# Mixing layer, second part: squares in place and shorter lags between its stages

## The chip, the cores and the metric

One core of a Trainium2 chip runs the whole program. The time is the device time of one execution in microseconds; the time of a kernel is the median of its runs. Engines: PE (TensorE, matrix products and transposes into PSUM), DVE (VectorE), ACT (ScalarE), POOL (GpSimd, no access to PSUM), and SP, which here only issues DMAs. Each engine runs its own list of instructions in order; semaphores tie them together.

## The reference

Four blocks follow each other on `x` (4096 tokens of 128 channels, as 4 sequences of 1024): `x = x + layernorm(block(layernorm(x)))`. The change lies in the first block, a mixing layer with a recurrence, and in the hand-over to the second, a mixture of 16 experts:

```
x = x + r * wkv                                # first part, recurrence over time
h2 = _ln(x, ln2_w, ln2_b)
xx2 = concatenate([h2[:, -1:], h2[:, :-1]])     # shift by one token
xxx2 = h2 + (xx2 - h2) * ts
kc = xxx2 @ Wck.T                              # 128 -> 512
rc = sigmoid(xxx2 @ Wcr.T)
vv = relu(kc) ** 2 @ Wcv.T                     # 512 -> 128
return x + rc * vv
```

Second block: `scores = sigmoid(x @ w_gate.T)`; the best two of four groups of experts, in them the best four experts, their scores normalised to weights; then every expert's `silu(x @ w1.T) * (x @ w3.T) @ w2.T`, weighted and summed, and a shared expert.

## The kernel before, in words

Tokens are worked in 8 groups of 512 (two groups to a sequence); matrices in work are 128 channels by 512 tokens, a PSUM bank each (8 banks). `X` and `XA` hold tokens by rows, `B[0..5]` six buffers of 128 x 4100 (`KF` = `B[2]` keys, `VF` = `B[3]` values, `RF` = `B[4]`, `XXX` = `B[1]`, `MMB` = `B[5]`), `RB` sixteen rows of 512 for short-lived results.

Each engine has a loop `for step in ...` in which a stage of group g runs at step g + lag; the order of the stages in a step is the order of the list of (lag, stage) pairs. "Round" below is one such step. The stages of the second part, with the lines of the profile:

- decay (DVE L870 to L875, ACT L1469 and L1472): exponents for group g from its keys; tanh and exp on ACT.
- wkv (DVE L881 to L898): scan and what follows; it reads the values `VF` and signals `y_b`. Group g + 1 needs group g.
- res: PE transposes y back (L344), DVE adds it to the tokens (L902) and takes the statistics (L799, L803; signals `st0`).
- rstd on POOL (L1769 to L1775; four dependent small instructions, the second a power), norm on ACT (L1413), turn on PE (L344) and ACT (L1476), and for every second group a copy of the last token on DVE (L911) that the shift of that sequence needs.
- mix (DVE L916, L918): shift and blend, signals `xxx_b`.
- kc: PE multiplies by four blocks of Wck and by Wcr (L392, five products; the profile shows two records each). ACT takes relu of the four (L1492) and squares chunks 1 and 3 (L1497), POOL squares chunks 0 and 2 (L1840), ACT takes tanh of the fifth (L1501). Relu goes to half of `B[KF]` (even and odd groups in turn), squares to half of `B[VF]`. Since both hold keys and values of all groups, group 0 waits for `y_b` 4 and group 1 for `y_b` 8.
- vv (PE L405): four products, accumulated. DVE multiplies by the gate (L925, `y2_b`).
- ret: transposed back (L344), added, with statistics (L930, L799); rstd on POOL; add: norm on ACT (L1413), added to `X` on POOL (L1801).
- the expert gate's norm: statistics (`stats_n`), rstd, norm to row 9 of `RB`, turn (PE L344, ACT L1516), gate (PE L428: 16 columns for each 128 tokens).

The choice of experts (`route`, DVE L979 to L1017) is cut into pieces by `yield`; it runs for three ranges of tokens, of which the first is groups 0 and 1, after `score_n` on ACT (L1521, sigmoid). Its weights are transposed on PE (L438), copied (`spread_n`, DVE L1023), sent by SP to DRAM and read back spread over partitions (128 KB a piece) into the four buffers `CW`. POOL's `gated_m` (L1872) multiplies a unit by its weights. A unit (`experts(v)`) is one expert for one group: `gate_up_m` (PE L447, L450), silu (ACT L1530), product (DVE L1037), `gated_m`, and three units later `out_m` (PE L462). Nine units make a group, 72 in all. Units begin at `FIRST_UNIT` = 20 of the loop and run alone after its end at step NG + 15 = 23. After the first four pieces SP also loads the weights and the tables of the third block (896 and 1024 KB) before the piece of unit 4.

The lags before, on PE: res 2, turn 4, kc 8, vv 9, ret 10, turn_n 14, gate_n 15. On DVE and ACT they match.

Of the kernel before, what the change touches and what calls it, by code (L numbers as in the profile page):

```python
# [64 lines left out]
def build(nc, I, out):  # L65
    ctx = ExitStack()
    with ctx:
# [84 lines left out]
        XF = 0  # L152
        small = [SS[:, 512 * i:512 * i + 512].rearrange("p (i e) -> p i e", e=16) for i in range(4)]
# [118 lines left out]
        FIRST_UNIT = 20  # L272
# [62 lines left out]
        def tensor_program():  # L335
# [50 lines left out]
            def kc_b(g):  # L386
                pe.wait_ge(s["xxx_b"], g + 1)
                for c in range(5):
# [21 lines left out]
            def ret_b(g):  # L410
                pe.wait_ge(s["y2_b"], g + 1)
                turned(room(0), lambda j: quarter(row(11), j), s["yt2_b"])
                banks.lend(0, s["xa2_b"], g + 1)

            def turn_n(g):
                pe.wait_ge(s["hn2"], g + 1)
                turned(room(1), lambda j: quarter(row(9), j), s["tp2"])
                banks.lend(1, s["xf_n"], g + 1)

            def gate_n(g):  # L420
                pe.wait_ge(s["xf_n"], g + 1)
                r = range_of(g)
                i = (2, 3, 0)[r]
# [9 lines left out]
            def cut_n(g):  # L433
                pe.wait_ge(s["cut_n"], range_of(g) + 1)
                i = 1 + g if g < 2 else next_d(0)
# [86 lines left out]
            for step in range(NG + 15):  # L522
                for lag, stage in ((15, gate_n), (14, turn_n), (10, ret_b), (9, vv_b), (8, kc_b), (4, turn_b), (2, res_b)):
# [7 lines left out]
            for v in range(NG + 15 - FIRST_UNIT, ALONE):  # L531
# [262 lines left out]
        def vector_program():  # L794
# [133 lines left out]
            def ret_b(g):  # L928
                dve.wait_ge(s["yt2_b"], g + 1)
                dve.scalar_tensor_tensor(tokens(XA, g), bank(0), 0.5, tokens(XA, g), ALU.mult,  # L930
# [145 lines left out]
            def experts(v):  # L1076
                if v == 2:
# [24 lines left out]
            for step in range(NG + 15):  # L1102
# [9 lines left out]
            for v in range(NG + 15 - FIRST_UNIT, ALONE):  # L1112
# [283 lines left out]
        def scalar_program():  # L1396
# [86 lines left out]
            def kc_b(g):  # L1483
                rl = B[KF][:, g % 2 * 2048:g % 2 * 2048 + 2048]
                sq = B[VF][:, g % 2 * 2048:g % 2 * 2048 + 2048]
                for c in range(4):
                    part = slice(512 * c, 512 * c + 512)
                    act.wait_ge(s["kc_b"], 5 * g + c + 1)
                    act.wait_ge(s["y_b"], 8 if g else 4)
                    if g >= 2:  # L1490
                        act.wait_ge(s["sqp_b"], 2 * g - 2)
                    act.activation(rl[:, part], bank(bank_of["kc", g, c]), ACT.Relu).then_inc(s["rl_b"], 1)  # L1492
                    if c % 2:
                        act.wait_ge(s["rl_b"], 5 * g + c + 1)
                        if g >= 2:
                            act.wait_ge(s["vv_b"], g - 1)
                        act.activation(sq[:, part], rl[:, part], ACT.Square).then_inc(s["sqa_b"], 1)  # L1497
# [10 lines left out]
            def norm_n(g):  # L1508
                if g:
                    act.wait_ge(s["tp2"], g)  # L1510
                normed(g, "n", x_tile, row(9), s["hn2"])
# [6 lines left out]
            def score_n(r):  # L1518
                first, count = RANGES[r]
                act.wait_ge(s["lg_n"], (first + count) // 4)  # L1520
                act.activation(flat(SC[:, first:first + count, :]), bank((2, 3, 0)[r])[:, 0:16 * count],  # L1521
# [60 lines left out]
            for step in range(NG + 15):  # L1582
                if step == 17:
                    score_n(0)
                if step == 19:
                    score_n(1)
                for lag, stage in ((14, turn_n), (13, norm_n), (11, add_b), (8, kc_b), (4, turn_b), (3, norm_b), (0, decay_b)):
                    if 0 <= step - lag < NG:
                        stage(step - lag)
                if step >= FIRST_UNIT:  # L1590
                    experts(step - FIRST_UNIT)
                    between_m(step - FIRST_UNIT)
            for v in range(NG + 15 - FIRST_UNIT, ALONE):
# [163 lines left out]
        def gpsimd_program():  # L1757
# [74 lines left out]
            def squares_b(g):  # L1832
                rl = B[KF][:, g % 2 * 2048:g % 2 * 2048 + 2048]
# [441 lines left out]
```

## Time and profile before

| | |
|---|---|
| Time, 3 runs | 1390.99 us median (1390.65 to 1392.84) |
| The profiled execution | 1394.51 us, span of its instructions 1393.1 us |
| Busy over the span | PE 1137.2 us (82%), DVE 1085.5 (78%), POOL 752.5 (54%), ACT 717.5 (52%) |
| Mean clock granted to PE | 0.902 of 2.4 GHz |
| The stretch the change touches | about 84 us (first wkv) to 252 us (first `out_m`) |

Times in rows of the trace are microseconds from the start of the span, mean durations included in the row are of one group of like instructions that follow each other ("x4" is four of them). The bracket at the end is the idle time of the engine before the row and what ended it.

### The profile page before, as it was taken

The numbers are of one execution on the slowest core, as the hardware profiler recorded it, in microseconds if no ns is written. First come the engines' busy times: TensorE is split into PE (matmuls) and PEld (weight loads), VectorE is DVE, ScalarE is ACT, GpSimd is POOL, SyncE is SP. The second block draws the span as 40 slices with busy tenths as digits, with TensorE's granted clock in tenths as the row PEclk, the third lists the DMA queues.
The fourth block names the chain that finished last, engine by engine and source line by source line (L and its number), as shares of the span: only waits on it lengthen the run. The fifth ranks groups of instructions, "written<-read, shape, count | busy, mean of one in ns | idle before, by whom it ended". The sixth has DMA issues, their size and how long they took to land.

```text
span 1393.1 us, 18719 instructions
## 1 busy us (share of the span) xinstructions
PE 1137.2 (82%) x5568; PEld 534.3 (38%) x5568; DVE 1085.5 (78%) x2974; ACT 717.5 (52%) x1535; POOL 752.5 (54%) x982
## 2 busy tenths in 40 slices
PE   3603798799999997777767769999999999999895
PEld 1202345455554554433422233344434433344232
DVE  5889655574788788788898859889999999999227
ACT  4644677236644335533231126676666666756781
POOL 7523485355787778855856015735562546254623
PEclk9855997999999998987785669999999999999998
DMA  4000100622111110001222231121201111100001
GB/s 118 0 0 0 51 1 0 151 84 65 61 39 45 46 38 23 0 0 26 49 48 42 40 56 28 19 50 19 38 16 24 30 27 24 17 4 1 4 8 54
DMA packets 33682, 47.02 MB, mean 34 GB/s; under 512 B 5023, under 2 KB 18207, under 8 KB 33279
## 3 DMA queue, kind: packets, MB, share of 16 engines
q1 hardware_dynamic: 30990, 43.84, 14.2%
q10 hardware_dynamic: 2592, 2.00, 0.5%
q8 instruction: 44, 0.72, 0.2%
q14 instruction: 56, 0.46, 0.1%
HBM read 39.14 MB, written 6.68 MB: 33 GB/s over the span
## 4 chain that ended last, share of the span: by engine, by line
PE 35%; DVE 17%; POOL 5%; ACT 3%; issue 3%; DMA 1%; ACTq 0%; POOLq 0%; DVEq 0%; SPq 0%
PE PS L710 9%; PE PS L639 7%; PE PS L693 6%; PE PS L756 4%; DVE PS L1209 3%; DVE RB L1143 3%; DVE SS L1212 3%; PE PS L344 2%; DVE st L799 2%; PE PS L545 1%; POOL SS L1978 1%; DVE PS L1123 1%; PE PS L564 1%; ACT RB L1694 1%; ACT SS L1736 1%
## 5 line engine op out<-in xcount | busy, mean ns | idle before, releaser
L1694 ACT ACTIVATE RB<-PS 128x512 f32<-128x512 f32 (+3 forms) x768 | 321.3, 500 | 161.5 <-PE PS L693 158.7
L639 PE MATMUL PS<-B 96*128 96x512 bf16 (+3 forms) x768 | 247.7, 349 | 36.4 <-DVE SS L1209 12.5
L1209 DVE CUSTOM_DVE_ANT_0 PS<-PS,w_msk 128x128 f32<-128x128 f32 (+3 forms) x512 | 242.3, 506 | 16.4 <-PE PS L639 16.0
L693 PE MATMUL PS<-B 96*128 96x512 bf16 (+3 forms) x768 | 231.0, 329 | 4.2 <-ACT RB L1694 2.9
L1212 DVE TENSOR_REDUCE SS<-PS 128x1 f32<-128x512 f32 x256 | 175.7, 686 | 37.6 <-PE PS L639 36.5
L2056 POOL TENSOR_SCALAR_AFFINE_SELECT RB<-RB 128x512 f32<-128x512 f32 x128 | 81.3, 640 | 225.8 <-ACT RB L1694 225.8
L710 PE MATMUL PS<-RB,B 128*32 128x512 f32 (+3 forms) x1536 | 164.6, 502 | 3.9 <-POOL RB L2056 3.9
L639 PEld LDWEIGHTS PS<-B 96*128 96x128 bf16 x768 | 74.8, 99 | 220.1 <-DVE SS L1209 94.7
L1872 POOL TENSOR_TENSOR RB<-RB,B 128x512 f32<-128x512 f32 x64 | 82.3, 1288 | 85.7 <-DVE RB L1037 61.6
L1530 ACT ACTIVATE RB<-PS 128x512 f32<-128x512 f32 x72 | 42.8, 596 | 124.1 <-PE PS L447 124.0
L693 PEld LDWEIGHTS PS<-B 96*128 96x128 bf16 x768 | 72.7, 98 | 76.9 <-ACT RB L1694 43.7
L462 PEld LDWEIGHTS PS<-B,RB 128*128 128x128 f32 x576 | 77.4, 197 | 42.3 <-issue 28.1
L1771 POOL TENSOR_TENSOR rs<-rs,mhalf 128x4 f32<-128x4 f32 (+1 forms) x67 | 88.0, 1313 | 5.6
L344 PE MATMUL PS<-w_ident,RB 128*128 128x128 f32 x256 | 43.7, 301 | 55.0 <-issue 21.5
L545 PE MATMUL PS<-B,WW 128*128 128x512 f32 x128 | 71.4, 686 | 18.8 <-DVE RB L1143 12.6
L462 PE MATMUL PS<-B,RB 128*128 128x128 f32 x576 | 79.0, 282 | 9.0 <-POOL RB L1872 8.9
L1037 DVE TENSOR_TENSOR RB<-RB,PS 128x512 f32<-128x512 f32 x72 | 48.8, 680 | 42.3 <-PE PS L450 15.9
L447 PE MATMUL PS<-B 128*128 128x512 f32 x144 | 77.6, 622 | 0.3 <-ACT RB L1530 0.3
L450 PE MATMUL PS<-B 128*128 128x512 f32 x144 | 75.0, 603 | 1.3 <-DVE RB L1037 1.3
L1209 DVE DVE_READ_ACCUMULATOR2_ANT SS<- 128x1 f32 x512 | 72.3, 141 | 0.0
L756 PE MATMUL PS<-WW,B 128*128 128x512 f32 x128 | 61.2, 615 | 0.9 <-DVE XA L1276 0.5
L1769 POOL TENSOR_SCALAR rs<-mv 128x4 f32<-128x4 f32 (+1 forms) x67 | 20.6, 308 | 73.7 <-DVE mv L803 70.4
(275 smaller groups left out, 2237.7 us busy)
## 6 DMA issues: line engine op xcount, KB each, us to landing
B<-scrW SPq DMA_DIRECT2D x128, 128.0 KB, 3.0
B<-scrQ SPq DMA_DIRECT2D x72, 128.0 KB
scrQ<-B SPq DMA_DIRECT2D x6, 384.0 KB, 2.6
B<-scrK SPq DMA_DIRECT2D x36, 64.0 KB
X<-in_x SPq DMA_DIRECT2D x8, 256.0 KB, 8.5
out_dram<-X SPq DMA_DIRECT2D x7, 256.0 KB, 3.2
B<-in_w SPq DMA_DIRECT2D x3, 576.0 KB, 4.7
B<-in_zeros SPq DMA_DIRECT2D x9, 128.0 KB
```

Of the source, the lines that this page charges most:

```text
L462: ins = pe.matmul(quarter(p, q), quarter(row(5 + n % 3), q), w2[:, j, :], start=(j == 0 and q == 0), stop=(j == 8), skip_group_check=True)
L545: ins = pe.matmul(bank(i + h), wvr[:, j - 1, :], cf(XF, 2 * b + h), start=True, stop=True)
L639: pe.matmul(p[:, 0:w], qs[u % 3][:, h, 128 * i:128 * i + 128], keys_of(u, h)[:, 512 * c:512 * c + w], start=True, stop=True).then_inc(s["m ...
L693: pe.matmul(p[:, 0:w], keys_of(u, 4 * kl + z)[:, 128 * kt:128 * kt + 128], qs[u % 3][:, 4 * kl + z, 512 * qc + off:512 * qc + 512], start= ...
L710: ins = pe.matmul(p[32 * j:32 * j + 32, off:off + w], VA[:, 8 * (u // 2) + kt, 2 * (u % 2) + kl, :], pb[:, j, 0:w], start=(kt == 0), stop= ...
L756: pe.matmul(room(i), quarter(cf(HB, g), j), wE[:, 4 * half:4 * half + 4, :].rearrange("p e c -> p (e c)"), start=True, stop=True).then_inc ...
L1209: ins = dve.tensor_tensor_reduce(p, p, msk[:, 512 - w:512], 1.0, LOWEST, ALU.add, ALU.max, MX[:, u % 2, i, h, c:c + 1])
L1212: ins = dve.tensor_reduce(MX[:, u % 2, i, h, c:c + 1], p, AX, ALU.max)
L1694: act.activation(RB[:, 4 * (step % 3) + z, 0:w], bank(bank_of["score", step, z])[:, 0:w], ACT.Exp).then_inc(s["ex2"], 1)
L1771: own.done(pool.tensor_tensor(R[:, s4, 0], R[:, s4, 3], mhalf[:, 0:count], ALU.pow))
L1872: pool.tensor_tensor(row(5 + n % 3), row(3 + j % 2), CW[m % 4], ALU.mult).then_inc(s["b_m"], 1)
L2056: pool.affine_select(out=pb, in_=pb, compare_op=ALU.is_ge, fill=0.0, base=0, pattern=[[0, 4], [1, 128]], channel_multiplier=-1).then_inc(s ...
```

## The change

- The squares are taken in place: relu of an even group goes to `SLOT[0]` = the first half of `B[KF]`, of an odd group to `SLOT[1]` = the first half of `B[VF]`. Chunk c of the first two groups waits for `y_b` c + 1; later groups wait for the vv product two groups back.
- Lags on PE: res 1, turn 2, kc (four products) 3, the fifth product and vv 4, ret 5, turn_n 9, gate_n 10. The order within a step is new on every engine.
- vv gets bank 2, ret bank 3, the gate logits of the first two ranges bank 0, of the third bank 2.
- The gate's norm is written to two halves of `WX` in turn instead of one row, and waits one group less.
- The loop ends at step NG + 10 = 18; the first unit is at step 14. The choice of the first range starts at step 12 with eight pieces a step; the transposes and the spreading of its weights stand ahead of unit 0 instead of unit 2; `score_n` for ranges 0 and 1 stands at steps 11 and 13.

```diff
+        SLOT = [B[z][:, 0:2048] for z in (KF, VF)]
-        FIRST_UNIT = 20
+        FIRST_UNIT = 14
+        B_STEPS = NG + 10
 # PE
-            def kc_b(g):
+            def kc_b(g, part=range(4)):
                 pe.wait_ge(s["xxx_b"], g + 1)
-                for c in range(5):
+                for c in part:
...
+            def kc_last(g):
+                kc_b(g, (4,))
             def vv_b(g):
-                sq = B[VF][:, g % 2 * 2048:g % 2 * 2048 + 2048]
-                i = next_bank()
+                sq = SLOT[g % 2]
+                i = 2
 # PE, experts(v)
-                if v == 2:
+                if v == 0:
                     cut_n(0)
                     cut_n(1)
 # PE, main loop
-            for step in range(NG + 15):
-                for lag, stage in ((15, gate_n), (14, turn_n), (10, ret_b), (9, vv_b), (8, kc_b), (4, turn_b), (2, res_b)):
+            for step in range(B_STEPS):
+                for lag, stage in ((9, turn_n), (5, ret_b), (10, gate_n), (4, kc_last), (2, turn_b), (1, res_b), (4, vv_b), (3, kc_b)):
 # DVE, main loop
-                for lag, stage in ((12, stats_n), (10, ret_b), (9, vv_b), (6, mix_b), (4, turn_b), (2, res_b),
-                                   (1, wkv_b), (0, decay_b)):
+                for lag, stage in ((1, wkv_b), (0, decay_b), (2, turn_b), (3, mix_b), (1, res_b), (4, vv_b), (5, ret_b), (7, stats_n)):
-                if step >= 18:
-                    for _ in range(4):
+                if step >= 12:
+                    for _ in range(8):
                         next(routes[0], None)
 # ACT
             def kc_b(g):
-                rl = B[KF][:, g % 2 * 2048:g % 2 * 2048 + 2048]
-                sq = B[VF][:, g % 2 * 2048:g % 2 * 2048 + 2048]
+                rl = SLOT[g % 2]
                 for c in range(4):
                     part = slice(512 * c, 512 * c + 512)
                     act.wait_ge(s["kc_b"], 5 * g + c + 1)
-                    act.wait_ge(s["y_b"], 8 if g else 4)
-                    if g >= 2:
-                        act.wait_ge(s["sqp_b"], 2 * g - 2)
+                    if g < 2:
+                        act.wait_ge(s["y_b"], c + 1)
+                    if c == 0 and g >= 2:
+                        act.wait_ge(s["vv_b"], g - 1)
...
-                        act.activation(sq[:, part], rl[:, part], ACT.Square).then_inc(s["sqa_b"], 1)
+                        act.activation(rl[:, part], rl[:, part], ACT.Square).then_inc(s["sqa_b"], 1)
-                for lag, stage in ((14, turn_n), (13, norm_n), (11, add_b), (8, kc_b), (4, turn_b), (3, norm_b), (0, decay_b)):
+                for lag, stage in ((9, turn_n), (4, kc_b), (2, turn_b), (0, decay_b), (6, add_b), (8, norm_n), (1, norm_b)):
 # POOL, main loop (before: rstd n 12, add 11, rstd r 10, squares 8, rstd b 2)
+            for step in range(NG + 8):
+                if 0 <= step - 4 < NG:
+                    squares_b(step - 4)
+                if 0 <= step - 8 < NG:
+                    rstd(step - 8, 1e-5, "n")
+                if 0 <= step - 6 < NG:
+                    add(step - 6, step - 5, row(15))
+                if 0 <= step - 1 < NG:
+                    rstd(step - 1, 1e-5, "b")
+                if 0 <= step - 5 < NG:
+                    rstd(step - 5, 1e-5, "r")
```

## Rows read from the trace of the kernel before

**Rows 1.** Windows: us, busy us (instructions) of PE, PEld, DVE, ACT, POOL, then PEclk, DMA share, GB/s

```profile
84.00:133.00 49.00, 10.74 (x40) 7.17 (x41) 45.70 (x101) 17.19 (x31) 19.19 (x20) 0.50 0.00 1
133.00:156.00 23.00, 15.05 (x34) 7.01 (x32) 17.98 (x41) 11.71 (x22) 9.76 (x10) 0.79 0.00 1
...
180.00:220.00 40.00, 39.68 (x131) 20.33 (x129) 20.89 (x95) 31.91 (x68) 31.25 (x50) 1.00 0.01 1
220.00:233.00 13.00, 8.23 (x47) 7.26 (x47) 7.89 (x51) 10.39 (x26) 10.34 (x20) 0.67 0.00 0
```

**Rows 2.** Timeline, DVE: one early round, 100 to 108 us (start, duration, engine, line)

```profile
100.04 0.66 DVE L881 TENSOR_TENSOR RB<-RB,B 128x512 f32<-128x512 f32 x1
...
104.84 0.68 DVE L870 TENSOR_TENSOR RB<-B 128x512 f32<-128x512 f32 x1
...
106.24 0.68 DVE L902 SCALAR_TENSOR_TENSOR XA<-PS,XA 128x512 f32<-128x512 f32 x1
...
108.02 0.66 DVE L881 TENSOR_TENSOR RB<-RB,B 128x512 f32<-128x512 f32 x1
```

**Rows 3.** Timeline, DVE: the mix of a group, and the product with the gate

```profile
124.17 0.68 DVE L916 TENSOR_TENSOR RB<-B 128x512 f32<-128x512 f32 x1
124.89 0.75 DVE L918 SCALAR_TENSOR_TENSOR B<-RB,w_vecs,B 128x512 f32<-128x512 f32 x1
...
200.67 0.69 DVE L925 SCALAR_TENSOR_TENSOR RB<-RB,PS 128x512 f32<-128x512 f32 x1 [1.56 <-PE PS L405]
```

**Rows 4.** Timeline, ACT: decay and norm early, then one group's activations

```profile
97.58 0.72 ACT L1469 ACTIVATE RB<-RB,dv 128x512 f32<-128x512 f32 x1 [6.12 <-DVE RB L870]
98.39 1.06 ACT L1472 ACTIVATE RB<-RB 128x1024 f32<-128x1024 f32 x1
99.35 1.63 ACT L1413 ACTIVATE HN<-XA,rs 128x128 f32<-128x128 f32 x4
...
144.58 1.07 ACT L1492 ACTIVATE B<-PS 128x512 f32<-128x512 f32 x2
...
148.33 0.77 ACT L1476 ACTIVATE B<-PS,w_vecs 128x512 f32<-128x512 f32 x1
```

**Rows 5.** Timeline, POOL: one rstd early, one later, and two squares

```profile
92.23 0.58 POOL L1769 TENSOR_SCALAR rs<-mv 128x4 f32<-128x4 f32 x1 [11.91 <-DVE mv L803]
...
95.64 0.67 POOL L1775 TENSOR_SCALAR rs<-rs 128x4 f32<-128x4 f32 x1
...
162.40 0.23 POOL L1769 TENSOR_SCALAR rs<-mv 128x4 f32<-128x4 f32 x1 [3.15 <-DVE mv L803]
...
164.13 0.25 POOL L1775 TENSOR_SCALAR rs<-rs 128x4 f32<-128x4 f32 x1
...
178.46 2.04 POOL L1840 TENSOR_TENSOR B<-B 128x512 f32<-128x512 f32 x2
```

**Rows 6.** Timeline, PE: the five kc products of groups 5 and 6

```profile
191.87 4.46 PE L392 MATMUL PS<-B,WW 128*128 128x512 f32 x10
...
200.47 4.45 PE L392 MATMUL PS<-B,WW 128*128 128x512 f32 x10
```

**Rows 7.** Timeline: from the last y2 to the gates of the first expert units

```profile
219.56 0.69 DVE L925 SCALAR_TENSOR_TENSOR RB<-RB,PS 128x512 f32<-128x512 f32 x1 [1.56 <-PE PS L405]
...
227.16 0.19 DVE L979 TENSOR_TENSOR SS<-SC 128x64 f32<-128x64 f32 x1
...
231.54 0.87 DVE L799 BATCH_NORM_STATS2 st<-X 128x6 f32<-128x128 f32 x4 [1.83 <-POOL X L1801]
...
238.31 0.29 DVE L1017 TENSOR_TENSOR SS<-SS 128x128 f32<-128x128 f32 x1
...
243.42 1.28 DVE L1023 COPY B<-PS 16x512 f32<-16x512 f32 x2 [0.49 <-PE PS L438]
...
250.62 1.26 POOL L1872 TENSOR_TENSOR RB<-RB,B 128x512 f32<-128x512 f32 x1 [15.86 <-DMA B<-scrW]
...
265.36 3.76 POOL L1872 TENSOR_TENSOR RB<-RB,B 128x512 f32<-128x512 f32 x3 [6.88 <-DMA B<-scrW]
```

More of the change, by code:

```diff
@@ L411, in ret_b @@
                 pe.wait_ge(s["y2_b"], g + 1)
-                turned(room(0), lambda j: quarter(row(11), j), s["yt2_b"])
-                banks.lend(0, s["xa2_b"], g + 1)
+                turned(room(3), lambda j: quarter(row(11), j), s["yt2_b"])
+                banks.lend(3, s["xa2_b"], g + 1)
             def turn_n(g):
                 pe.wait_ge(s["hn2"], g + 1)
-                turned(room(1), lambda j: quarter(row(9), j), s["tp2"])
+                turned(room(1), lambda j: quarter(WX[:, 512 * (g % 2):512 * (g % 2) + 512], j), s["tp2"])
                 banks.lend(1, s["xf_n"], g + 1)
@@ L530, in tensor_program @@
                     between_m(step - FIRST_UNIT)
-            for v in range(NG + 15 - FIRST_UNIT, ALONE):
+            for v in range(B_STEPS - FIRST_UNIT, ALONE):
                 experts(v)
@@ L1100, in between_m @@
                     head_d(g, k)
-            for step in range(NG + 15):
-                for lag, stage in ((12, stats_n), (10, ret_b), (9, vv_b), (6, mix_b), (4, turn_b), (2, res_b),
-                                   (1, wkv_b), (0, decay_b)):
+            for step in range(B_STEPS):
+                for lag, stage in ((1, wkv_b), (0, decay_b), (2, turn_b), (3, mix_b), (1, res_b), (4, vv_b), (5, ret_b), (7, stats_n)):
                     if 0 <= step - lag < NG:
                         stage(step - lag)
-                if step >= 18:
-                    for _ in range(4):
+                if step >= 12:
+                    for _ in range(8):
                         next(routes[0], None)
@@ L1111, in vector_program @@
                     experts(step - FIRST_UNIT)
-            for v in range(NG + 15 - FIRST_UNIT, ALONE):
+            for v in range(B_STEPS - FIRST_UNIT, ALONE):
                 experts(v)
@@ L1580, in between_m @@
                     add_m((v - 5) // 9)
[L1582 to L1586, printed above, removed]
-                for lag, stage in ((14, turn_n), (13, norm_n), (11, add_b), (8, kc_b), (4, turn_b), (3, norm_b), (0, decay_b)):
+            for step in range(B_STEPS):
+                for lag, stage in ((9, turn_n), (4, kc_b), (2, turn_b), (0, decay_b), (6, add_b), (8, norm_n), (1, norm_b)):
                     if 0 <= step - lag < NG:
                         stage(step - lag)
+                if step == 11:
+                    score_n(0)
+                if step == 13:
+                    score_n(1)
                 if step >= FIRST_UNIT:
@@ L1592, in scalar_program @@
                     between_m(step - FIRST_UNIT)
-            for v in range(NG + 15 - FIRST_UNIT, ALONE):
+            for v in range(B_STEPS - FIRST_UNIT, ALONE):
                 experts(v)
@@ L1839, in squares_b @@
                     pool.wait_ge(s["rl_b"], 5 * g + c + 1)
-                    pool.tensor_tensor(sq[:, part], rl[:, part], rl[:, part], ALU.mult).then_inc(s["sqp_b"], 1)
-            for step in range(NG + 12):
-                if 0 <= step - 12 < NG:
-                    rstd(step - 12, 1e-5, "n")
-                if 0 <= step - 11 < NG:
-                    add(step - 11, step - 10, row(15))
-                if 0 <= step - 10 < NG:
-                    rstd(step - 10, 1e-5, "r")
-                if 0 <= step - 8 < NG:
-                    squares_b(step - 8)
-                if 0 <= step - 2 < NG:
-                    rstd(step - 2, 1e-5, "b")
+                    pool.tensor_tensor(rl[:, part], rl[:, part], rl[:, part], ALU.mult).then_inc(s["sqp_b"], 1)
+            for step in range(NG + 8):
+                if 0 <= step - 4 < NG:
+                    squares_b(step - 4)
+                if 0 <= step - 8 < NG:
+                    rstd(step - 8, 1e-5, "n")
[5 more added lines that the diff above has]
+                    rstd(step - 5, 1e-5, "r")
             def head_d(g, k):
```

23 lines of the change are left out of this document (9 added, 14 removed).

## The prediction

> **What bounds the kernel now.** I first cut the stretch that the change touches into windows [rows 1]. From 84 to 133 us VectorE (DVE) is busy 45.7 of 49.0 us, TensorE (PE) 10.7, and PE's clock is at its lower level, 1.2 GHz (0.50). From 180 to 220 us it is the reverse: PE is busy 39.7 of 40.0 us at 2.4 GHz (1.00) and DVE 20.9. So the second part of the mixing layer is two phases one after the other: a recurrence bound by DVE with PE empty, then products bound by PE with DVE half empty. The cause is in the code: the squares of a group lie in the value buffer, so the activations of group 1 wait until the recurrence has read all eight groups. Behind both comes a tail, 220 to 233 us, in which PE is busy 8.2 of 13.0 us at a mean clock of 0.67. Last I read that tail in order of time [rows 7]: the last y2 starts at 219.56, the choice of the first range runs from 227.16 to 238.31, the transposed weights are spread at 243.42, go through DRAM, and free POOL's first expert unit at 250.62 after 15.86 us of waiting.
>
> **The change, part by part.** I follow one round (a step of the loops) on each engine.
>
> DVE. An early round takes 7.98 us (100.04 to 108.02): wkv 4.80, decay 1.40, residual with its statistics 1.78 [rows 2]. A full round adds mix (0.68 + 0.75, together 1.4) and the product with the gate, 0.7 [rows 3], the return, made of the same forms as the residual, 1.8, and the gate norm's statistics, 1.8 less 0.7 = 1.1. That is 13.0 us with all of it, 11.9 without the last.
>
> ACT. A group's activations run from 144.58 to 148.33, 3.8 us, then turn 0.77; decay is 0.72 + 1.06 and each of the three norms 1.63 [rows 4]. Together with the 0.6 us of the gate's turn this is 3.8 + 0.8 + 1.8 + 4.9 + 0.6 = 11.9 us, under DVE's 13.0.
>
> PE. Two neighbouring groups start their kc products 8.6 us apart while PE is full [rows 6], so a group costs 8.6 us at 2.4 GHz and, by doubling, some 17 at 1.2 GHz. At the upper level it fits under DVE's round.
>
> POOL. An rstd beside wkv runs from 92.23 to 96.31, 4.1 us; beside statistics it runs from 162.40 to 164.38, 2.0; two squares take 2.04 [rows 5]. With three rstds, one of them slow, the squares, and an add that I put at 1.3 (a square with two inputs, rounded up), a round is 2.0 + 2.0 + 4.1 + 2.0 + 1.3 = 11.4 us: also under 13.0, but not by much.
>
> Squares in place cost nothing: the same eight instructions a group, other addresses. Their price is the wait of the next group but one for vv, which lies two rounds back. The other banks and the norm's own buffer take waits away and add none. No DMA is added. The three weight loads wait for the last y_b, which comes later now (about 170 instead of 156 us), and are wanted at the first unit past 205: still hidden.
>
> The new order. Round 1 ends its residual at 92 us and round 2 at 100, as now. Lag 1 puts the norm of a group into the round of its residual, so the rstd (4.1), norm (1.6), turn (about 1.1 on slow PE and 0.8 on ACT) and decay (1.8) follow in one chain: 9.9 us from one end of statistics to the next but one exp. Round 3 so waits 1.9 us and ends at 111.3 (100.0 + 1.9 + 8.0 + 1.4). Round 4 is the first with kc: PE's residual transposes stand behind the fifth kc product and the turn, on a slow PE, and I put its end at 124, and the first vv at 127. From there DVE sets the pace: 124, 138 (11.9 and 2 for that vv), then 13 each (11.9 or 13.0, up to 1 for waits on hf and for POOL beside DVE): 151, 164, and round 8 ends at 177.
>
> Then DVE is no longer the bound. Round 9 waits for the last norm: rstd 3.7 with what stands ahead of it on POOL, norm 1.7, the gate's turn 0.6, activations 3.8, turn 0.8, mix 1.4, together 12; the kc of group 6 and its activations 6.5, two norms and a turn 3.9, the activations of group 7 to their last square 3.6, and the last vv product 0.9. Sum 27, so the last vv ends at 204, and I add 2 for stretches of PE at the lower clock: 206, where it now ends at 219.5.
>
> The tail. y2 0.7, return of group 6 1.8, statistics 1.1, return of group 7 1.8, statistics 1.1, the choice, statistics 1.1. The choice spans 227.16 to 238.60 with 1.83 us idle and one 1.1 us set of statistics in it [rows 7], so it is itself 8.5 us. Sum 16.1; with the transposes of the weights 17.5. The spread then starts at 223.5 instead of 243.42: 19.9 us earlier. I take this as the gain, since the first gates hang on it alone: by the same rows POOL's gate of unit 4 stands at 265.36 behind a 6.88 us DMA wait, 21.9 us after the spread, and PE has until then for four more units beside the last norms. So **20 us off**. From unit 4 the program is the same.
>
> The profiled execution took 1394.5 us with a span of 1393.1; the median of the three runs is 1391.0, 3.5 below. A difference carries over: 1391.0 - 20 = 1371.0.
>
> **The clock, weighed.** The mean clock was 0.67 from 220 to 233 us, where PE worked in pieces with pauses between them [rows 1]. The new rounds have such pauses too; if the clock falls in them as it did there, at worst 1.2 us for each of the six rounds from the sixth on is lost beyond my 2, and the gain is 13 instead of 20. The Trainium skill, "TensorE: Matmul & The Clock Gate", section "HAM oscillation — how this bites in real kernels", asks only that PE not idle for long at one stretch; by that rule the 2 us pieces that I see between transposes and vv cost nothing and the gain would be 22.
>
> **The rivals.** (A) As above. Its own range is 14 us (the clock row) to 27 us off (rounds of 12.0, no clock loss): 1364 to 1377.
>
> (B) POOL and ACT set the pace. For it: an rstd beside wkv is twice as long [rows 5], and the change puts two or three of them a round into the recurrence, while norm, turn, decay and activations now stand in one order on ACT. With all rstds at 4.1 and squares at 1.3 a round on POOL is 12.3 + 2.6 + 1.3 = 16.2 us. Rounds 5 to 8 then end 13 us later, of which round 9 gives back 3 (its rstd has waited already): 10 off, 1381. The Trainium skill, "GPSIMD Engine Reference", section "1. Specifications", says that POOL shares its SBUF interfaces with VectorE where VectorE reads two SBUF inputs, which wkv does; by that rule the stretch is real and DVE's own rows would lengthen too. Against it: most rstds fall beside PSUM reads and statistics.
>
> (C) No change. If PE's work, merely moved, ran at 1.2 GHz up to the last groups, rounds 4 to 11 would take 14.3 us each: 111.3 + 8 x 14.3 = 225.7, plus 17.5 = 243.2, today's time. 1391.
>
> (D) Slower. PE's clock stays at its lower level. Its queue holds the residual's transposes behind kc and the turn; DVE waits for them before it can go on, so PE idles in turn, at 1.2 GHz with 17 us of work a round. Rounds of 17 from the fourth give 111.3 + 8 x 17 = 247.3, plus 17.5 = 264.8: 21 us slower, 1412. It decides once a round passes 14.3 us. For it: 0.50 from 84 to 133 us. Against it: 0.79 from 133 to 156 us, where kc and vv begin [rows 1].
>
> **How the numbers follow.** A has 0.66, B 0.19, C 0.06, D 0.09. The predicted time is A's, 1371. The range holds A and most of B: from 1363 to 1384, leaving out C, D and the ends. About 0.2% (2.8 us) is what a measurement of this kernel can tell from no change; faster by more is A and B, 0.85, within it 0.06, slower 0.09.
>
> **What would show it.** Right: kc products from about 110 us on; the last y_b at 165 to 175 instead of 155.7; rounds of 12 to 13.5 us between 124 and 177; PE's clock above 0.8 from 125 us on; the last vv at 200 to 210; the spread near 223 and POOL's wait for the weights ahead of unit 0 no longer in PE's way. Wrong: rounds over 14.3 us; DVE idle for the residual's transposes by more than 1 us a round; a clock of 0.5 to 0.6 past 130 us; the spread at its place but a new wait ahead of unit 4.

## The result and the profile after

The changed kernel takes 1382.3 us (median of 6 runs, 1374.6 to 1384.2) beside 1393.15 us for the kernel before in the same series (6 runs, 1390.7 to 1397.2): the medians are 10.9 us apart. The ratio is 0.9909 (interval 0.9882 to 0.9937), which is 12.7 us less. Set against the 1391.0 of the prediction the ratio gives 1378.3; both this and the raw median lie inside the range of 1363 to 1384, and they are 7 and 11 us above the predicted 1371.0. The profiled execution took 1384.16 us with a span of 1382.8 (before 1394.51 and 1393.1), 10.3 less.

The profile page of the kernel after, its span and its busy time:

```profile
span 1382.8 us, 18688 instructions
...
PE 1134.7 (82%) x5568; PEld 531.9 (38%) x5568; DVE 1089.8 (79%) x2974; ACT 716.7 (52%) x1535; POOL 751.0 (54%) x982
```

The work is the same as before (PE was 1137.2 busy, DVE 1085.5, POOL 752.5); what changed is when it is done. The windows of the kernel after (us, busy us and instructions of PE, PEld, DVE, ACT, POOL, then PEclk, DMA share, GB/s):

```profile
84.00:133.00 49.00, 21.52 (x69) 11.99 (x70) 42.29 (x86) 23.81 (x44) 18.16 (x20) 0.68 0.00 1
133.00:156.00 23.00, 17.07 (x51) 7.86 (x49) 22.45 (x58) 12.31 (x24) 14.13 (x17) 1.00 0.00 1
156.00:178.00 22.00, 16.41 (x44) 8.58 (x45) 19.48 (x50) 16.82 (x36) 16.94 (x21) 0.81 0.09 24
178.00:190.00 12.00, 11.17 (x33) 5.34 (x32) 3.84 (x24) 7.00 (x15) 6.63 (x12) 0.93 0.26 105
190.00:212.00 22.00, 21.11 (x71) 10.37 (x69) 9.89 (x42) 16.63 (x37) 15.79 (x26) 1.00 0.01 2
212.00:230.00 18.00, 8.49 (x46) 7.63 (x47) 16.98 (x94) 13.88 (x31) 12.24 (x24) 0.65 0.00 0
230.00:252.00 22.00, 21.77 (x96) 13.31 (x94) 11.42 (x37) 9.97 (x17) 6.78 (x8) 0.90 0.78 182
```

Beside [rows 1]: PE now works 21.5 us in the recurrence's first stretch instead of 10.7, and DVE is busy 22.45 of 23.0 us from 133 to 156. But from 190 to 212 PE is full (21.1 of 22.0 at 2.4 GHz) and DVE has 9.9 us of work. The phase bound by PE is shorter, not gone. The timeline of DVE shows it by the products with the gate (y2) of groups 2 to 7, and then the start of the choice:

```profile
150.28 0.65 DVE L930 SCALAR_TENSOR_TENSOR RB<-RB,PS 128x512 f32<-128x512 f32 x1
...
165.26 0.69 DVE L930 SCALAR_TENSOR_TENSOR RB<-RB,PS 128x512 f32<-128x512 f32 x1 [0.97 <-PE PS L410]
...
181.02 0.69 DVE L930 SCALAR_TENSOR_TENSOR RB<-RB,PS 128x512 f32<-128x512 f32 x1 [2.71 <-PE PS L410]
...
191.53 0.68 DVE L930 SCALAR_TENSOR_TENSOR RB<-RB,PS 128x512 f32<-128x512 f32 x1
...
201.91 0.69 DVE L930 SCALAR_TENSOR_TENSOR RB<-RB,PS 128x512 f32<-128x512 f32 x1 [5.51 <-PE PS L410]
...
211.84 0.69 DVE L930 SCALAR_TENSOR_TENSOR RB<-RB,PS 128x512 f32<-128x512 f32 x1 [6.42 <-PE PS L410]
...
218.05 0.19 DVE L984 TENSOR_TENSOR SS<-SC 128x64 f32<-128x64 f32 x1
```

The last y2 is 7.7 us earlier than the 219.56 of [rows 7]. Behind it the hand-over to the experts, again in order of time in the kernel after:

```profile
229.96 0.68 DVE L1028 COPY B<-PS 16x512 f32<-16x512 f32 x1
...
237.47 1.27 POOL L1871 TENSOR_TENSOR RB<-RB,B 128x512 f32<-128x512 f32 x1 [5.55 <-DMA B<-scrW]
...
252.73 3.76 POOL L1871 TENSOR_TENSOR RB<-RB,B 128x512 f32<-128x512 f32 x3 [6.66 <-DMA B<-scrW]
...
254.05 1.37 PE L467 MATMUL PS<-B,RB 128*128 128x128 f32 x8 [2.28 <-POOL RB L1871]
...
255.21 1.91 PE L452 MATMUL PS<-B 128*128 128x512 f32 x2
...
256.91 1.70 PE L455 MATMUL PS<-B 128*128 128x512 f32 x2
```

The row at 229.96 is the spread (the copy of the transposed weights), the row at 237.47 the gate of unit 0 (the product of a unit with its weights, on POOL), and the row at 252.73 begins with the gate of unit 4. From the last y2 to the spread it is 18.1 us, before 23.9; so the spread is 13.5 us earlier. The gate of unit 4 is 12.6 earlier (265.36 to 252.73): 22.8 us behind the spread instead of 21.9. Then PE, which has waited 2.28 us, runs the next unit's products at 1.2 GHz (1.91 and 1.70 us; the kernel before ran them at 267.67 in 1.02 after a wait of 2.50), which costs 1.7 more. At unit 34 the product stands at 348.2 instead of 359.2, 11.0 us earlier, and that is what the end shows. So of the 19.9 us forecast 5.8 are missing at the last y2, 0.6 in the tail (18.1 for 17.5), 0.9 between spread and gate, and 1.7 in the clock: 9.0, which leaves 10.9.

### The profile page after: what moved, and what is told of

Its sections match the earlier page's. It is cut to its first block, busy times and chain, and to the rows that moved or that the text cites. A ratio compares the mean times of both kernels' runs of the same rounds, so it can differ in the third digit from the quotient of the medians.

```text
span 1382.8 us, 18688 instructions
## 1 busy us (share of the span) xinstructions
PE 1134.7 (82%) x5568; PEld 531.9 (38%) x5568; DVE 1089.8 (79%) x2974; ACT 716.7 (52%) x1535; POOL 751.0 (54%) x982
## 4 chain that ended last, share of the span: by engine, by line
PE 35%; DVE 17%; POOL 5%; ACT 3%; issue 3%; DMA 1%; ACTq 0%; POOLq 0%; DVEq 0%; SPq 0%
PE PS L715 9%; PE PS L644 7%; PE PS L698 6%; PE PS L761 4%; DVE PS L1213 3%; DVE RB L1147 3%; DVE SS L1216 3%; PE PS L346 2%; DVE st L804 2%; PE PS L550 1%; POOL SS L1977 1%; DVE PS L1127 1%; ACT RB L1696 1%; PE PS L569 1%; DVE B L1147 1%
## 5 line engine op out<-in xcount | busy, mean ns | idle before, releaser
L644 PE MATMUL PS<-B 96*128 96x512 bf16 (+3 forms) x768 | 247.6, 349 | 36.2 <-DVE SS L1213 12.6
L2055 POOL TENSOR_SCALAR_AFFINE_SELECT RB<-RB 128x512 f32<-128x512 f32 x128 | 81.0, 637 | 226.1 <-ACT RB L1696 226.1
L1773 POOL TENSOR_TENSOR rs<-rs,mhalf 128x4 f32<-128x4 f32 (+1 forms) x67 | 84.5, 1261 | 5.6
L550 PE MATMUL PS<-B,WW 128*128 128x512 f32 x128 | 71.5, 687 | 18.8 <-DVE RB L1147 12.6
L346 PE MATMUL PS<-w_ident,RB 128*128 128x128 f32 x224 | 36.4, 287 | 39.8 <-issue 21.5
L1897 POOL TENSOR_TENSOR RB<-RB 128x1024 f32<-128x1024 f32 x16 | 38.1, 2381 | 40.4 <-DVE RB L1147 40.2
```

What stands on the lines that cost most here:

```text
L550: ins = pe.matmul(bank(i + h), wvr[:, j - 1, :], cf(XF, 2 * b + h), start=True, stop=True)
L644: pe.matmul(p[:, 0:w], qs[u % 3][:, h, 128 * i:128 * i + 128], keys_of(u, h)[:, 512 * c:512 * c + w], start=True, stop=True).then_inc(s["m ...
L1773: own.done(pool.tensor_tensor(R[:, s4, 0], R[:, s4, 3], mhalf[:, 0:count], ALU.pow))
L2055: pool.affine_select(out=pb, in_=pb, compare_op=ALU.is_ge, fill=0.0, base=0, pattern=[[0, 4], [1, 128]], channel_multiplier=-1).then_inc(s ...
```

## The experiments

Twelve kernels ran, in three series, each beside the kernel before on the same chip. "Last y2" is the start of the last product with the gate (L930 or its like), "spread" that of the first copy of the transposed weights, "gate of unit 4" that of its product on POOL, "unit 34" that of its DVE product; the kernel before has 219.6, 243.4, 265.4 and 359.2.

| | median us | ratio (interval) | last y2 | spread | gate of unit 4 | unit 34 |
|---|---|---|---|---|---|---|
| k0 the change again | 1380.5 | 0.9905 (0.9885 to 0.9925) | 213.6 | 231.7 | 253.6 | 347.4 |
| k1 old hand-over | 1393.9 | 1.0003 (0.9988 to 1.0018) | 211.2 | 241.6 | 261.0 | 354.9 |
| k1b old hand-over, scores kept | 1391.7 | 0.9989 (0.9974 to 1.0003) | 210.5 | 237.8 | 258.6 | 355.0 |
| k2 hand-over only | 1389.5 | 0.9964 (0.9946 to 0.9981) | 219.4 | 236.1 | 258.1 | 353.7 |
| k3 squares in place only | 1392.8 | 0.9986 (0.9969 to 1.0003) | 219.3 | 240.5 | 262.2 | 357.7 |
| k4 ACT's order | 1378.6 | 0.9903 (0.9875 to 0.9932) | 212.6 | 230.7 | 250.1 | 344.0 |
| k5 earlier choice | 1379.1 | 0.9897 (0.9876 to 0.9918) | 213.2 | 226.1 | 248.8 | 342.6 |
| k6 all squares on ACT | 1381.6 | 0.9919 (0.9901 to 0.9937) | 210.8 | 228.9 | 250.0 | 343.8 |
| k7 = k4 + k5 | 1380.7 | 0.9900 (0.9874 to 0.9926) | 215.7 | 228.7 | 250.9 | 344.8 |
| k8 later transfers | 1376.4 | 0.9871 (0.9845 to 0.9897) | 211.1 | 229.3 | 246.7 | 344.9 |
| k9 = k4 + k5 + k8 | 1381.9 | 0.9909 (0.9885 to 0.9934) | 216.8 | 229.8 | 249.4 | 345.9 |
| k10 before + later transfers | 1390.6 | 0.9962 (0.9941 to 0.9983) | 221.3 | 242.4 | 259.2 | 355.6 |

The kernel before had medians of 1392.8 (k0 to k3), 1393.9 (k1b, k4 to k6) and 1394.6 (k7 to k10). The landmarks come from one profiled execution each, and they carry over to the medians only roughly: k4 and k5 lead by 15.2 and 16.6 us at unit 34 and by 15 in the median, but k6 leads by 15.4 there and by 12 in the median. The two profiles of the changed kernel itself differ as much: in k0 the last y2 is 1.8 us later, unit 34 is 0.9 earlier, and the whole execution is 5.6 us shorter (1378.6 and 1384.2). And where the order of the transfers is the same, the gate of unit 4 comes 19.4 (k1, k4) to 22.8 us (the first profile) behind the spread. So 2 or 3 us at one landmark of one execution decide nothing.

### The change again (k0)

> The changed kernel once more, as the mark for the three beside it. 9 to 13 us below the kernel before; last vv product at 210 to 213 us, spread of the weights at 229 to 231. If the first measurement was a lucky one, less than 6 us.

1380.5 us, ratio 0.9905: the gain is confirmed at 11 to 13 us. The last y2 is at 213.6 here and at 211.8 in the first profile. The two part in the fourth round: PE's fifth kc product and the transposes behind it take 1.70 and 1.06 us in k0, 1.10 and 0.60 in the first profile (granted clock from 120 to 122 us 0.55 and 1.00), so DVE waits 1.73 us for the residual's transposes instead of 0.30, and the residual starts at 123.3 instead of 121.9. This spread of 1.8 us between executions of the same kernel is to be kept in mind below.

### The parts: old hand-over (k1, k1b), hand-over alone (k2), squares in place alone (k3)

```diff
 # k1, from the kernel after; k1b has the steps of score_n as after
-        FIRST_UNIT = 14
+        FIRST_UNIT = 15
-                if v == 0:      # cut_n and spread_n, on PE and DVE
+                if v == 2:
-                if step >= 12:
-                    for _ in range(8):
+                if step >= 13:
+                    for _ in range(4):
-                if step == 11:
+                if step == 12:
                     score_n(0)
-                if step == 13:
+                if step == 14:
                     score_n(1)
```

> New lags and squares in place, but the hand-over to the experts in its old place (choice from one step later, four pieces a step, weights turned ahead of unit 2). Theory (the two parts add): the last vv stays at 212 us, the spread comes 23 to 24 us behind it as before the change (235 to 236 instead of 230), and PE waits 6 to 8 us ahead of the first out product: 5 to 6 us of the gain are lost, about 5 us below the kernel before. Rival (the gain is all in the lags; the units ahead of the first out product only fill a hole that is paid either way): as the changed kernel, 10 us below.

With the new lags and the old hand-over nothing is left: 1.0003, where the theory had 5 us and the rival 10. The last y2 is early (211.2), but the spread falls back to 241.6. The timeline of PE in k1 shows a wait that the kernel before does not have:

```profile
221.24 1.86 PE L433 MATMUL PS<-w_gate,B 128*128 128x16 f32 x8 [7.34 <-ACT SC L1523]
```

The later score of the first range holds bank 0, which the second range's gate needs. That is a fault of this experiment and not of the old hand-over, so k1b kept the scores at steps 11 and 13.

> As the run with the old hand-over, but the two scores stay at their steps 11 and 13, so that the gate of the second range need not wait for the first scores to leave bank 0. Theory (that wait of 7.3 us at 221 us held the whole tail in the first attempt): the last vv stays at 211, the spread comes some 24 us behind it at 235 to 236 instead of 241.6, and the kernel is 4 to 6 us below the kernel before. Rival (the wait only moved idle time): spread at 240 or later, within 2 us of the kernel before.

PE's longest wait at L433 is now 0.59 us, the spread comes at 237.8, and the time is still 0.9989: about the rival's 2 us, though neither spread was met (235 to 236 in the theory, 240 or later in the rival). Two rows of k1b, the gate of unit 0 and PE's first `out_m`:

```profile
246.13 1.26 POOL L1871 TENSOR_TENSOR RB<-RB,B 128x512 f32<-128x512 f32 x1 [18.30 <-DMA B<-scrW]
...
247.45 2.08 PE L467 MATMUL PS<-B,RB 128*128 128x128 f32 x8 [7.50 <-POOL RB L1871]
```

The choice, in small pieces and called out at `v == 2`, ends late, the tail from last y2 to spread is 27.3 us instead of 18.1, and PE stands 7.5 us for the first gated unit (6.4 in the kernel before). A lead of 9 us at the last y2 becomes 4.2 at unit 34.

```diff
 # k2, from the kernel before
-        FIRST_UNIT = 20
+        FIRST_UNIT = 19
-                if v == 2:      # cut_n and spread_n
+                if v == 0:
-                if step >= 18:
-                    for _ in range(4):
+                if step >= 17:
+                    for _ in range(8):
```

(with `score_n` at steps 16 and 18, behind the stages)

> The lags before and squares in their own buffer, with only the hand-over moved up (first unit at step 19, choice from step 17, eight pieces a step, weights turned ahead of unit 0). Theory: last vv at 219.5 as before, spread 18 us behind it at 237 to 238, 5 to 6 us below the kernel before. Rival: the choice in one piece on DVE delays the last norms by as much, and unit 0 starts no earlier where it matters: within 2 us of the kernel before.

Ratio 0.9964, which is 5.0 us (3.3 by the medians); spread 16.7 us behind the last y2, gate of unit 4 7.2 us earlier, unit 34 5.5 earlier: near the theory. So the hand-over alone is worth 3 to 5 us, the lags with the old hand-over 0 to 4 (4.2 at unit 34 in k1b, 1.5 by its ratio, with an interval that holds no change), and both together 11 to 13: the parts do not add up. The lags only bring y2 forward; what the rest of the kernel sees is the spread.

```diff
 # k3, from the kernel before: SLOT and kc_b, vv_b, squares_b as in the change, all lags as before
+        SLOT = [B[z][:, 0:2048] for z in (KF, VF)]
+                    if g < 2:
+                        act.wait_ge(s["y_b"], c + 1)
+                    if c == 0 and g >= 2:
+                        act.wait_ge(s["vv_b"], g - 1)
```

> The lags and the hand-over before, with only the squares in place. Theory (the buffer's wait is what kept the two phases apart, but at lag 8 little can use its absence): the activations of group 1 no longer wait for the last y_b, PE's waits of 7.2 us at 145 and about 1 us at 156 shrink, and the last vv comes 3 to 6 us earlier; 3 to 6 us below the kernel before. Rival (at lag 8 the old lags alone set the order): within 1 us of the kernel before.

No difference that can be told (0.9969 to 1.0003), as the rival had it. The squares in place are free, as forecast, and by themselves they bring nothing: PE's wait at 145 us, 7.18 in the kernel before, is still 6.74. By the code they are what allows the lags, since group 1 would wait for the last `y_b` otherwise; the new lags without them were not run.

### What sets the last rounds: ACT's order (k4) and POOL's squares (k6)

First the timeline of PE in the kernel after, from the end of the recurrence:

```profile
175.20 0.66 PE L346 MATMUL PS<-w_ident,RB 128*128 128x128 f32 x4 [3.79 <-DVE RB L903]
...
175.69 5.29 PE L410 MATMUL PS<-B,WW 128*128 128x512 f32 x8
...
180.82 3.60 PE L394 MATMUL PS<-B,WW 128*128 128x512 f32 x8
...
191.67 3.70 PE L394 MATMUL PS<-B,WW 128*128 128x512 f32 x8 [0.58 <-DVE B L923]
...
195.21 0.60 PE L346 MATMUL PS<-w_ident,WX 128*128 128x128 f32 x4
...
196.08 0.96 PE L433 MATMUL PS<-w_gate,B 128*128 128x16 f32 x8
...
197.07 1.10 PE L394 MATMUL PS<-B,WW 128*128 128x512 f32 x2
...
198.20 3.67 PE L410 MATMUL PS<-B,WW 128*128 128x512 f32 x8
...
201.71 3.60 PE L394 MATMUL PS<-B,WW 128*128 128x512 f32 x8
```

PE starts the kc of groups 5, 6 and 7 at 180.82, 191.67 and 201.71: three groups were still owed when the last residual ended at 178. One costs 10.0 us (10.8 for group 5, with waits of 0.83 and 0.58 in it): kc's four products 3.5, two turns 0.9, gate 1.0, fifth product 1.1, vv 3.5. The question was whether PE sets this pace, or ACT, whose relu (L1496) of group 7 at 206.27 stands behind the gate's turn (L1518).

```diff
 # k4, ACT's main loop, from the kernel after
-                for lag, stage in ((9, turn_n), (4, kc_b), (2, turn_b), ...
+                for lag, stage in ((4, kc_b), (9, turn_n), (2, turn_b), ...
```

> ACT takes the activations of kc ahead of the gate's turn in each round. Theory (in rounds 9 to 11 the relus wait for a transpose that PE does only after all four kc products, so vv, kc, turn and relu run one after the other, 10 us a round): the relus follow the products, rounds 10 and 11 fall from 10.4 and 9.9 to about 9.2 us, round 9 ends 2 to 3 us earlier, and the last vv comes 3 to 5 us earlier; 13 to 18 us below the kernel before. Rival (ACT's own work sets these rounds): last vv within 1 us of 212, 11 to 13 us below.

The last y2 moves only from 213.6 (k0, whose path up to the recurrence's end is the same) to 212.6, as the rival had it; the time, 1378.6, lies in the theory's range but cannot be told from k0. PE's timeline in k4:

```profile
177.45 5.30 PE L410 MATMUL PS<-B,WW 128*128 128x512 f32 x8
...
193.08 3.60 PE L394 MATMUL PS<-B,WW 128*128 128x512 f32 x8
...
199.40 3.67 PE L410 MATMUL PS<-B,WW 128*128 128x512 f32 x8
...
202.91 3.60 PE L394 MATMUL PS<-B,WW 128*128 128x512 f32 x8
```

From kc to kc it is still 9.8 us, without a wait of over 0.1 us between. So ACT's order costs 0.5 us a round, and what is left of rounds 10 and 11 is PE's own work, not ACT's as the rival said. In both kernels a vv runs partly at 1.2 GHz (5.29 and 5.30 us instead of 3.6) after PE has waited 3.8 us for wkv.

```diff
 # k6, from the kernel after: ACT squares all four chunks, POOL's squares_b leaves the loop, vv waits for ACT alone
-                    if c % 2:
-                        act.wait_ge(s["rl_b"], 5 * g + c + 1)
-                        act.activation(rl[:, part], rl[:, part], ACT.Square).then_inc(s["sqa_b"], 1)
+                    act.wait_ge(s["rl_b"], 5 * g + c + 1)
+                    act.activation(rl[:, part], rl[:, part], ACT.Square).then_inc(s["sqa_b"], 1)
```

> All four squares on ACT, none on POOL. Theory A (POOL's squares lengthen DVE's instructions in the rounds of the recurrence, five to seven rows by 0.7 us, and stand ahead of vv): rounds 5 to 8 shorten by 0.5 to 1 us each, last vv 2 to 3 us earlier, 13 to 15 us below the kernel before. Theory B (ACT is nearly full in these rounds, 11.9 us of work before, 13.1 now): each round from 5 to 11 grows by 0.5 to 1.2 us, last vv 4 to 8 us later, 4 to 8 us below the kernel before.

Both theories missed. In k6 the fifth y2 is at 177.2, 3.8 us before that of the kernel after; the last is at 210.8, only 1.1 before. Four rows of k6, one of POOL and three of PE (the vv of group 4, the fifth kc product of group 5, the kc of group 6), show where the lead was won and lost:

```profile
176.87 1.27 POOL L1799 TENSOR_TENSOR X<-X,RB 128x512 f32<-128x512 f32 x1 [2.01 <-ACT RB L1414]
```

```profile
173.60 3.60 PE L407 MATMUL PS<-B,WW 128*128 128x512 f32 x8
...
183.05 1.10 PE L394 MATMUL PS<-B,WW 128*128 128x512 f32 x2 [1.54 <-ACT B L1493]
...
189.91 3.70 PE L394 MATMUL PS<-B,WW 128*128 128x512 f32 x8 [1.73 <-DVE B L920]
```

Of the 3.8 us 2.1 come from the recurrence (vv at 173.60 instead of 175.69; the two executions are level up to round 4, with the residual at 121.7 and 121.9) and 1.7 from the clock, since this vv takes 3.60 us and not 5.29. The loss falls mostly in round 9, and there PE is not the bound: it is busy 8.7 of 12.0 us from 178 to 190 (11.2 in the kernel after) and waits for ACT and for the mix. POOL's add waits 2.01 us for ACT, so the last norm's rstd starts at 178.23, hardly before the 178.41 of the kernel after, and ACT has two squares more to do. The kc of group 6 starts 1.8 us before that of the kernel after. So k6 says that ACT has no room for these squares, and nothing of PE's backlog.

Where the 2.1 us were won shows in rows of DVE and POOL. First the kernel after, one wkv beside POOL's squares:

```profile
170.66 2.48 POOL L1839 TENSOR_TENSOR B<-B 128x512 f32<-128x512 f32 x2
...
170.69 1.55 DVE L894 TENSOR_TENSOR RB<-B,SS 128x512 f32<-128x512 f32 x1
...
172.27 1.41 DVE L897 SCALAR_TENSOR_TENSOR RB<-RB 128x512 f32<-128x512 f32 x1
```

Then the same two rows of DVE in k6, with no squares on POOL:

```profile
169.88 0.69 DVE L891 TENSOR_TENSOR RB<-B,SS 128x512 f32<-128x512 f32 x1
...
170.60 0.69 DVE L894 SCALAR_TENSOR_TENSOR RB<-RB 128x512 f32<-128x512 f32 x1
```

They take 0.69 us each instead of 1.55 and 1.41, and POOL's pair of squares is stretched too (2.48 us; 2.04 in [rows 5]). The Trainium skill, "SBUF — State Buffer", section "SBUF: two separate sides", says that DVE operations with two SBUF inputs and POOL take turns at one pair of ports, each for a whole instruction; these rows agree.

### The hand-over: earlier choice (k5) and later transfers (k8)

```diff
 # k5, from the kernel after
-        FIRST_UNIT = 14
-        B_STEPS = NG + 10
+        FIRST_UNIT = 13
+        B_STEPS = NG + 9
 # PE: gate_n at lag 9, behind turn_b (was 10)
 # DVE: seven pieces of the choice ahead of vv_b in step 11
+                    if step == 11 and stage is vv_b:
+                        for _ in range(7):
+                            next(routes[0], None)
 # ACT: score_n at steps 10 and 12
```

> The gate of a group stands in the same round as its turn, the scores of the first range one round earlier, seven pieces of the choice ahead of the last product with the gate on DVE (where DVE waits 6.4 us for vv), first unit at step 13. Theory (the tail's length of 18 us from the last vv to the spread is the choice itself, 8.5 us on DVE, plus what stands ahead of it): the spread comes 9 to 11 us behind the last vv, at 221 to 224; the pieces of the units then wait for PE's slow clock and the last norms, and 5 to 7 us are gained on the changed kernel: 16 to 20 us below the kernel before. Rival (the chain of norms to the last gate is the bound, not the choice): 11 to 13 us below, as the changed kernel.

The spread comes 13.0 us behind the last y2 instead of 18.1 (at 226.1, forecast 221 to 224), 5.6 us before that of k0; the gate of unit 4 and unit 34 (342.6) are 4.8 us before those of k0. An earlier spread carries on to the units nearly one for one. The time is 1379.1, ratio 0.9897: 14 to 15 us below the kernel before, between what the theory (16 to 20) and the rival (11 to 13) had, and k0 and k5 cannot be told apart by their times.

```diff
 # k8, SP's queue, from the kernel after (k10: the same from the kernel before)
             sp.wait_ge(s["vv_b"], 8)
             sp.dma_start(WW[:, :, :], I["wL1"]).then_inc(s["w_ww"], 16)
             sp.dma_start(cs, I["rope"]).then_inc(s["w_cs"], 16)
 # these three lines moved from ahead of the loop over m to m == 10 within it
```

> The kernel after, with the transfers of the head's weights (896 KB) and of the rope table (1024 KB) issued behind the pieces of units 4 to 9 and no longer ahead of unit 4's. Theory 1 (GpSimd's gate of unit 4 waits for its piece of weights because 1.9 MB lie ahead of it in the queue): the wait of 6.7 us ahead of gate 4 goes or falls under 1, gate 4 comes 4 to 6 us earlier (247 to 249), the pieces of 128 KB land in 2 to 3 us, product of unit 34 3 to 5 us earlier, time 3 to 5 us less than the kernel after on the same chip. Theory 2 (units are then bound by TensorE or VectorE at once, and the wait only moves to them): gate 4 earlier, but unit 34 within 1 us of where it was, time within 1.5 us. Theory 3: the transfers collide with the pieces of units 10 to 14 instead, a wait of 4 to 6 us there, nothing gained.

Theory 1 holds in the trace. Two gates of POOL in k8:

```profile
246.68 1.26 POOL L1871 TENSOR_TENSOR RB<-RB,B 128x512 f32<-128x512 f32 x1 [1.48 <-DVE RB L1042]
...
249.72 1.26 POOL L1871 TENSOR_TENSOR RB<-RB,B 128x512 f32<-128x512 f32 x1 [1.79 <-DVE RB L1042]
```

The gate of unit 4 comes at 246.68, 6.0 us before that of the kernel after (where it is the first of the three in the row at 252.73), and waits 1.48 us for DVE, not 6.66 for a transfer; PE runs its units 2.6 us apart without a pause and at 2.4 GHz. Unit 34 is 3.3 us earlier, and the time, 1376.4 at a ratio of 0.9871, is the lowest of all kernels here: 4.1 us under k0 by the medians. The two ran in different series, and their intervals overlap (0.9845 to 0.9897 and 0.9885 to 0.9925), so the time alone does not settle it. The Trainium skill, "DMA: Bandwidth & Descriptors", section "Queues, rings and completion order", has each DMA engine take its descriptors in ring order; the wait that goes when 1.9 MB are issued later agrees.

> The kernel before with the later transfers alone. In it units 1 to 4 are also late because of them (the gate of unit 0 waits 15.9 us for its piece, that of unit 4 6.9 us). Theory 1 (the loads set the early units in both kernels alike): gate of unit 4 about 5 us earlier than 265.4, time 3 to 5 us less than the kernel before. Theory 2 (no bound): within 1.5 us. If theory 1 holds here and not with the change, the change's gain was partly taken by these loads.

The same edit on the kernel before gives 0.9962 (0.9941 to 0.9983; 4.0 us by the medians) and puts the gate of unit 4 6.2 us earlier (259.2). These transfers were in the way of both kernels alike, so they do not explain the missing part of the gain; the prediction passed them by because they cancel.

### Put together (k7, k9)

> The kernel after, with ScalarE's kc_b ahead of turn_n and the choice one round earlier, both at once. Theory 1 (rounds 9 to 11 are TensorE's own work, and the choice is worked beside them by VectorE, so the two gains lie on different engines): last y2 near 212, spread near 225, gate of unit 4 near 247, product of unit 34 18 us ahead of the kernel before, time 1376 to 1379, ratio near 0.989. Theory 2 (each edit fills the same gap, so that one takes the other's place): spread 226 to 230, unit 34 at 343 to 344, time no less than with either alone (1379 and 1380).

> The three edits together (ScalarE's order, earlier choice, later transfers). If the three gains are separate: spread near 225, gate of unit 4 near 242, product of unit 34 21 to 23 us ahead of the kernel before, time 1373 to 1376, ratio near 0.986. If the transfers only hid the wait of the units for TensorE: as with the first two edits, 1376 to 1379, ratio 0.989.

k7 came out near the numbers of its theory 2 (spread 228.7, unit 34 344.8, 1380.7), k9 above both of its ranges (1381.9). In both the last y2 moves back, to 215.7 and 216.8, and k9 is no better than the kernel after. PE's timeline in k7:

```profile
198.47 1.06 PE L433 MATMUL PS<-w_gate,B 128*128 128x16 f32 x8 [1.17 <-ACT B L1521]
...
199.38 5.38 PE L410 MATMUL PS<-B,WW 128*128 128x512 f32 x8
...
211.10 1.06 PE L433 MATMUL PS<-w_gate,B 128*128 128x16 f32 x8 [1.17 <-ACT B L1521]
```

The edits collide. k5 has the gate of group g in the step of its turn; k4 puts ACT's copy of that turn behind kc. So PE stands twice 1.17 us for ACT (L1521) with the vv queued behind, and one vv takes 5.38 us; the granted clock of k7 was 0.66 from 199 to 204 us. In k9 such a wait lasts 2.65 us, and the vv behind it, at 188.50, takes 6.43 us. k4 together with k8 alone, without the earlier gate, was not tried.

## Why the prediction was right or wrong

**Bound and direction: right.** The backlog of products moved under the recurrence and the end of the second part came forward. By k3 the squares in place cost nothing; but the cause that the prediction read from the code, the buffer, was only half of it, since without that wait and with the old lags nothing moved.

**Rounds 3 to 8: right.** The residuals of rounds 3 to 8 end at 113.3, 123.7, 137.0, 150.3, 164.2 and 178.2, forecast 111.3, 124, 138, 151, 164, 177. Rounds of 13.3 to 14.0 were forecast at 13; the rest is DVE rows stretched beside POOL's squares (1.6 us in round 8) and DVE's waits of about 1 us in rounds 7 and 8. The row that signals the last y_b starts at 174.45 (165 to 175).

**Rounds 9 to 11: the term that failed.** The sum put 12 us on round 9, 15 on what follows up to the last vv, and 2 on stretches at the lower clock: 29. Measured are 33.6 us (178.2 to 211.8). The mix of group 6 ends at 191.6, 13.4 after the recurrence instead of 12; from there 20.2 us follow instead of 15. The sum followed one chain from engine to engine as if PE were free. It was not. A row of DVE in the kernel after, the mix of group 7, and one of PE in the kernel before, the kc that follows those of [rows 6]:

```profile
195.64 0.75 DVE L923 SCALAR_TENSOR_TENSOR B<-RB,w_vecs,B 128x512 f32<-128x512 f32 x1
```

```profile
209.92 4.45 PE L392 MATMUL PS<-B,WW 128*128 128x512 f32 x10
```

Group 7 was mixed at 196.4, but PE started its kc only at 201.71, after 10.0 us of work: the kc and vv of group 6, and between them two turns and a gate. The price of 8.6 came from a pair without the gate; the next pair of the same trace has it and stands 9.4 us apart (200.47 to 209.92). That k4 took 9.8 us from kc to kc without a wait in PE shows that these two rounds are PE's own work. No run made that work shorter, so what it would give is not measured.

The 1.4 us of round 9 are of another kind, and here the cause is argued from one trace: the vv of group 4 took 1.7 us more at the lower clock, and the kc of group 5 and the gate's turn stood behind it, for which ACT waited:

```profile
184.89 0.60 ACT L1518 ACTIVATE B<-PS 128x512 f32<-128x512 f32 x1 [2.77 <-PE PS L346]
```

That is what the 2 us for the clock were meant for. With 1.2 for the late end of round 8 the sum is 1.2 + 1.4 + 5.2 - 2 = 5.8 us, more than half of the 9.0 missing.

**The tail: right.** 17.5 forecast, 18.1 measured. That it depended on the hand-over's edits was not said; k1b shows that without them it is 27.3 and that no gain can be told.

**"The first gates hang on it alone": nearly.** The gate of unit 4 came 22.8 us behind the spread (21.9). The 1.7 us that PE then lost at 1.2 GHz was not foreseen. PE's wait for that gate is one for a transfer, and k8 takes it away.

**The clock: between its two values.** On the path it cost 1.7 us at one vv after a wait of 3.8 us, and 1.7 at the products of a unit after one of 2.28: 3.4 us. The prediction had put 2; the rule by which pauses cost nothing, 0; the worst case by the row of [rows 1], 9.2 (2 and six times 1.2). So neither the rule nor the worst case held, and neither alone explains the missing 9.0.

**Slips in the working.** The chain of round 3 is put at 9.9 us, but its terms add up to 9.4; the round ended at 113.3 and not 111.3. A's own range ends at 14 us off, though the clock row gives 13. Neither changes the forecast by more than 1 us. Of the signs named, rounds of up to 14.0 us (12 to 13.5) and the last vv at 211.8 (200 to 210) came out just beyond their bounds, and the spread at 230.0 (223) by 7 us. PE's wait ahead of unit 4 was no new one (2.28 us, 2.50 before).

**The rivals.** B gave 1381, close to the result, but not for its reason: POOL is busy 14.1 of 23.0 and 16.9 of 22.0 us in the recurrence, rounds stayed at 14.0 and under, and taking the squares off POOL (k6) brought the last residual 2.4 us forward, not 13. Its side remark that DVE's own rows would lengthen is right. C and D needed PE at 1.2 GHz past 133 us; the clock was 1.00 from 133 to 156 and 0.81 from 156 to 178. A's mechanism held, and its size was off by half.

## What to carry to other kernels

When work is moved beside a phase bound by another engine, ask how much of it that engine's end still leaves: sum what each engine owes after the phase, not one chain across engines. A lead in the middle of a kernel is worth what the next hand-over lets through: here the new lags gave 0 to 2 us with the old hand-over (k1b), the new hand-over 3 to 5 with the old lags (k2), and both together 11 to 13. Large transfers that nobody wants yet belong behind the small ones that somebody waits for (about 4 us by the medians in either kernel; clear of noise in k10).

## What was not expected of the hardware

- PE fell to 1.2 GHz after a wait of 2.28 us in the kernel after (1.91 and 1.70 us for products of 1.02), and not after one of 2.50 us at the same place in the kernel before. In k7 a vv ran partly at 1.2 GHz after a wait of 1.17 us (5.38 us), and the vv behind the next wait of 1.17 us did not (3.68 us at 212.01). Each time the granted clock had been 1.00 in the stretch before. Why one fell and the other did not stays open.
- DVE's operations on two SBUF inputs took 1.41 to 1.55 us instead of 0.69 beside POOL's squares of whole tiles; beside POOL's small power (1.45 us instead of 1.04) three rows of DVE at 154.65 to 156.10 stayed at 0.69. Two rows with a single SBUF input (TENSOR_SCALAR at 145.71 and 158.50) were stretched beside the squares as well, to 1.15 and 1.26 us from 0.43 and 0.42.
